# The order of value products and scores on TensorE in two attention layers with narrow heads

## The chip, the cores and the metric

The kernel is one program on one core of a Trainium2 chip. The metric is the device time in microseconds of one execution. Three runs of the kernel before took 1552.82, 1553.26 and 1553.35 us; the median is 1553.26.

## The reference

The input x is 32 sequences of 64 tokens of 256 values, and a context of the same shape. Four layers follow one another:

- L0: two cross-attentions with 16 heads of 128 values, with layer norms and residuals, then a feed-forward stage of 1024 (gelu).
- L1: cross-attention in which the keys and values come from the context and x together (128 per sequence), 16 heads of 16 values, with a mask; then an RMS norm and a feed-forward stage.
- L2: layer norm, cross-attention to the context (64 keys), 16 heads of 16 values, with a mask; then layer norm and feed-forward.
- L3: a non-local block over all tokens with a norm over the whole batch.

The two layers with narrow heads are L1 and L2. For each of them, cut to what matters:

```
q, k, v = x @ wq + bq, h @ wk + bk, h @ wv          # 16 heads of 16
scores  = where(mask, q k^T, -big) * scale
w       = softmax(scores)
x       = (w v) @ wo + bo (+ residual)
```

Most products are computed in three passes: each float32 operand is split into a high and a low part of a faster format, and the products high-high, high-low and low-high are added (`split3`).

## The kernel before, in words

Each engine runs its own program, written out in order; semaphores join them. The function `narrow(layer, ...)` writes the part of all engines for L1 and L2. Its work is cut into units. In layer 1 a unit is one sequence (NU = 32 units, 128 keys), in layer 2 it is two sequences (NU = 16, 64 keys each). A half is 256 tokens: four units in layer 1, two in layer 2 (UH). The counter r is the place of a unit in its half.

What happens to unit u, in order of its data:

1. `pe_scores(e, u)` on TensorE: four small matmuls write the mask into the four score banks (L1609), then the products of queries and keys are added (L1616). It waits for the subtraction of unit u-1 (`sub_done`), since the banks are the same.
2. VectorE takes the maximum (L1869) and subtracts it (L1873).
3. ScalarE takes the exponential (L1760).
4. VectorE sums (L1843) and takes the reciprocal (L1846), one unit later in its program.
5. POOL multiplies (L1986).
6. `pe_transpose(e, u)` on TensorE turns the probabilities into banks 4 and 5 (L1631), in the loop two units later. It waits for POOL, for the copy of the unit before out of these banks, and for each bank until its last other user is evicted.
7. ScalarE copies them out (`act_probs`, L1782); its semaphore is `p_copied`.
8. `pe_values(e, u)` on TensorE multiplies them with the values (L1648), three units later. It waits for `p_copied` of its unit and for `lo_done` of the unit before.
9. ScalarE and VectorE split the result into a high part (`act_hi`, L1796) and a low part (`dve_lo`, L1838).
10. The output product of two such units (layer 1) or of one (layer 2), and its eviction into x_sb on VectorE (L1832).

Between these, TensorE computes the projections of the halves ahead (queries q, keys kc or k0 and k1, values v), the output products ("out") and transposes of the next norm ("norm"). These are the uses of a table that `Slots` keeps: `uses_of[u]` lists those of unit u in order, and `pe_use` issues one. Each has a bank; it waits until the use before in that bank is evicted, and a use in one of the banks of the transposes (4, 5) waits also for `p_copied` of unit u-3 (`turned`). In layer 1 the banks of the uses are 7 and 5 in turn, so k0, a norm and mostly "out" come to bank 5; in layer 2 "out" takes bank 4 (in units 9, 14 and 15 bank 7). The three-pass products of all uses have the line L175. `n_ahead` is the number of uses that the loop issues in the first group: 3 in layer 1, which is all of them, and 1 in layer 2. In layer 1 the uses are q, k0 at r=0; k1, out at r=1; v, and in some units norm, at r=2; v, out at r=3. In layer 2 they are mostly kc, out, q at r=0 and v, out, sometimes norm, at r=1.

ScalarE's order in unit u: evictions of the first group of uses, `act_hi(u-3)`, the other early evictions, the exponential of u, late evictions (q of layer 2 among them, L1713), `act_probs(u-2)`, parts of the norm. VectorE's order in unit u: maximum and subtraction of u, in layer 2 `dve_lo(u-3)`, the eviction of "out", sum and reciprocal of u-1, in layer 1 `dve_lo(u-3)`, parts of the norm.

Behind the loop come the last units, mixed with the feed-forward stage's first products.

Of the kernel before, what the change touches and what calls it, by code (L numbers as in the profile page):

```python
# [86 lines left out]
def build(nc, wpack, ctxT, ctx_tok, x_in, mask1, mask2, cols_in, rows_in, vb_in, out, spill):  # L87
    ctx = ExitStack()
    with ctx:
# [70 lines left out]
        def wait(e, sem, n):  # L160

            if n > 0:
                e.wait_ge(sem, n)
# [1230 lines left out]
        def narrow(layer, norm, nxt, qb, kb, vb, out_row, mask, before, behind, then):  # L1394
# [118 lines left out]
            def out_of(use):  # L1513

                if use[0] == "norm":
                    return use[1].s["ev"].sem, use[1].s["ev"].at(use[2] * KT + use[3])
                return (A_out if use[0] in slots.ON_ACT else V_out), slots.emptied[use]
# [7 lines left out]
            def values_banks(w):  # L1525

                return BP if own or w < NU - 3 else (6, 7)
# [67 lines left out]
            def pe_scores(e, u):  # L1595
                h, r = u // UH, u % UH
                if r == 0:
                    e.wait_ge(*out_of(("q", h)))
                    e.wait_ge(*out_of(("k1" if own else "kc", h)))
                if u == 0:  # L1600
                    e.wait_ge(mask_ready, layer)
                    e.wait_ge(before.sem, before.at(NCH - 1))
                else:
                    e.wait_ge(sub_done, u)
                for j in range(G // KT):
                    cells = ps[:, j, 0:KT * P].rearrange("p (k n) -> p k n", k=KT)
                    i, at = u // (NU // 4), u % (NU // 4) * UB * SEQ
                    keys = maskb[PW * j:PW * j + 4, at:at + UB * SEQ]
                    e.matmul(cells[:, :, 0:UB * SEQ], sel[PW * j:PW * j + 4, i:i + 1].to_broadcast([4, P]),  # L1609
                             keys.rearrange("p (a n) -> p a n", a=1).to_broadcast([4, KT, UB * SEQ]),  # L1610
                             start=True, stop=False, skip_group_check=True)
                for k in range(KT):
                    for b in range(UB):
                        for j in range(G // KT):
                            at, rows_j = k * P + b * nk, slice(PW * j, PW * (j + 1))
                            ins = e.matmul(ps[:, j, at:at + nk],  # L1616
                                           qz[h % 2][rows_j, k, r * UB + b, :, :].rearrange("p h n -> p (h n)"),
                                           kT[h % 2][rows_j, k, r * UB + b, :], start=False, stop=True, skip_group_check=True)
                ins.then_inc(S_done, 1)

            def pe_transpose(e, u):
                e.wait_ge(nrm_done, u + 1)
                wait(e, p_copied, u)
                for half in range(2):
                    use = slots.last_in(BT[half], min(u + 2, NU))
                    if use is not None:
                        e.wait_ge(*out_of(use))
                    if BT[half] in BP:
                        wait(e, lo_done, min(u, NU - 3))
                    for n in range(4):  # L1630
                        ins = e.transpose(ps[:, BT[half], n * P:(n + 1) * P], t[u % 3][:, 4 * half + n, :], ident)  # L1631
                ins.then_inc(T_done, 1)

            def pe_values(e, u):
                h, r = u // UH, u % UH
                e.wait_ge(p_copied, u + 1)
                wait(e, lo_done, u)
                if u == 0:
                    e.wait_ge(*out_of(("row",)))
                e.wait_ge(*out_of(("v", h, r // 2 if own else 0)))  # L1640
                if not own and u == NU - 3:
                    e.wait_ge(*out_of(("out", last_outs[NU])))
                for k in range(KT):
                    for half in range(2):
                        for b in range(UB):
                            for j in range(G // KT):
                                rows_b = slice(b * nk, (b + 1) * nk)
                                ins = e.matmul(ps[j * PW:(j + 1) * PW, values_banks(u)[b], k * SEQ:(k + 1) * SEQ],  # L1648
                                               v[h % 2][half][rows_b, r, k * P + j * PW:k * P + (j + 1) * PW],
                                               pt[rows_b, j * KT + k, half * SEQ:(half + 1) * SEQ],  # L1650
                                               start=half == 0, stop=half == 1, skip_group_check=True)
                ins.then_inc(P_done, 1)
# [7 lines left out]
            def pe(e):  # L1660
                for use in uses_of[-1][1:]:
                    pe_use(e, -1, use)
                for u in range(NU):
                    pe_scores(e, u)
                    for use in uses_of[u][:n_ahead]:
                        pe_use(e, u, use)
                    if u >= 3:
                        pe_values(e, u - 3)
                    for use in uses_of[u][n_ahead:]:
                        pe_use(e, u, use)  # L1670
                    if u >= 2:
                        pe_transpose(e, u - 2)
                e.wait_ge(sub_done, NU)
                for use in uses_of[NU]:
                    pe_use(e, NU, use)
                then.lead(e)
                pe_transpose(e, NU - 2)
                pe_values(e, NU - 3)
# [304 lines left out]
            def pool_normalise(e, w):  # L1983
# [7 lines left out]
                          for f in range(7)}  # L1991
            behind[FT - 2] = Parts(pe_first, nothing, nothing if own else dve_columns, None)
            return load_mask, Parts(pe, act, dve, pool)

        next0, next1, next2, tail0, tail1, tail2 = Next(), Next(), Next(), {}, {}, {}
# [467 lines left out]
```

## Time and profile before

| what | value |
|---|---|
| median of three runs | 1553.26 us |
| span of the profiled execution | 1550.8 us |
| TensorE matmul (PE) busy | 1517.9 us |
| TensorE weight load (PEld) busy | 1304.4 us |
| VectorE (DVE) busy | 974.2 us |
| ScalarE (ACT) busy | 855.8 us |
| POOL busy | 402.3 us |

The profiled execution has no other time than its span of 1550.8 us, which is 2.5 us below the median of the runs. The trace puts the narrow layers at 1019.75 to 1167.21 us (the units of layer 1) and 1274.55 to 1367.46 us (those of layer 2). A row of a timeline gives start and length in us, the engine and line, how many instructions were merged, and in brackets how long the engine was idle before and which instruction ended that. The length of a matmul row has the drain of its last product in it, so that the next row can start before it ends.

### The profile page before, as it was taken

The page shows a single profiled execution, that of the slowest core. Times are in us where ns is not written, and L with a number is a line of the kernel's source. Part 1 is how long each engine was busy: PE and PEld are TensorE (multiplying, and loading weights), DVE is VectorE, ACT ScalarE, POOL GpSimd, SP SyncE. Part 2 cuts the span into 40 slices and gives each one's busy share as a digit, 9 for nine tenths or more (in the row PEclk, how much of TensorE's full clock was granted, in tenths as well). Part 3 has the DMA queues.
Part 4 walks back from the last instruction along what each step waited for, and adds up shares of the span by engine and source line. Part 5 has one row for each costly group of instructions (what it writes and reads, how often), then busy time and mean ns, then how long its engine had stood idle before and what let it go on. Part 6 is the DMA issues. An engine that isn't in the chain of part 4 may idle for free. (4 is left out here: it accounts for less than half of the span.)

```text
span 1550.8 us, 41283 instructions
## 1 busy us (share of the span) xinstructions
PE 1517.9 (98%) x17264; PEld 1304.4 (84%) x17264; DVE 974.2 (63%) x2115; ACT 855.8 (55%) x1610; POOL 402.3 (26%) x422
## 2 busy tenths in 40 slices
PE   8999999999999999999999999999999999999996
PEld 7888888888888888888888888978878988888864
DVE  7755555555577555555555576479996558865366
ACT  5553453453455453443443566576777567765476
POOL 1231011011033011101201123036764206542052
PEclk9999999999999999999999999999999999999998
DMA  6010010010010010010100000020002000000001
GB/s 229 2 70 2 29 43 1 29 42 1 29 42 2 29 42 1 29 43 1 31 27 29 28 2 28 1 84 2 3 29 83 1 28 3 31 2 28 8 22 55
DMA packets 17688, 46.20 MB, mean 30 GB/s; under 512 B 1344, under 2 KB 11600, under 8 KB 14560
## 3 DMA queue, kind: packets, MB, share of 16 engines
q1 hardware_dynamic: 13312, 39.33, 7.4%
q10 hardware_dynamic: 4192, 4.24, 0.8%
q8 instruction: 137, 2.24, 0.6%
q14 instruction: 47, 0.39, 0.1%
HBM read 39.37 MB, written 4.19 MB: 28 GB/s over the span
## 5 line engine op out<-in xcount | busy, mean ns | idle before, releaser
L175 PE MATMUL ps<-ch,W 128*128 128x512 f32 (+1 forms) x2484 | 596.5, 386 | 1.4 <-ACT arena L1725 0.6
L175 PEld LDWEIGHTS ps<-ch,W 128*128 128x128 f32 x2484 | 432.6, 188 | 87.5 <-issue 2.2
L175 PEld LDWEIGHTS ps<-W,split_arena 128*128 128x128 f32 x3084 | 392.6, 188 | 25.7 <-issue 4.2
L175 PE MATMUL ps<-W,split_arena 128*128 128x256 f32 x3084 | 406.5, 283 | 3.5 <-DVE split_arena L1226 2.4
L175 PE MATMUL ps<-W,ch 128*128 128x512 f32 (+1 forms) x864 | 203.5, 384 | 0.3
L892 ACT ACTIVATE arena<-ps 64x256 f32<-64x256 f32 x256 | 97.0, 379 | 187.8 <-PE ps L791 184.8
L991 DVE TENSOR_REDUCE small<-ps 128x4 f32<-128x260 f32 x128 | 54.1, 422 | 221.1 <-PE ps L720 221.0
L175 PEld LDWEIGHTS ps<-W,ch 128*128 128x128 f32 x864 | 151.6, 188 | 28.4 <-ACT arena L1713 0.9
L952 ACT ACTIVATE arena<-ps,hbias 128x512 f32<-128x512 f32 x128 | 87.8, 688 | 119.2 <-PE ps L175 118.3
L1226 DVE TENSOR_TENSOR split_arena<-arena,split_arena 128x512 fp32r<-128x512 f32 x96 | 71.9, 749 | 125.4 <-ACT split_arena L1258 113.8
L930 ACT ACTIVATE arena<-arena 128x260 f32<-128x260 f32 x128 | 54.3, 425 | 142.0 <-DVE arena L994 142.0
L1986 POOL TENSOR_TENSOR arena<-arena,small 128x1024 f32<-128x1024 f32 x48 | 94.9, 1979 | 126.9 <-DVE small L1846 126.9
L1255 ACT ACTIVATE arena<-ps,cols 128x512 f32<-128x512 f32 x96 | 65.9, 687 | 92.7 <-PE ps L175 92.7
L984 DVE SCALAR_TENSOR_TENSOR split_arena<-ps,hbias,split_arena 128x256 fp32r<-128x256 f32 x256 | 105.6, 474 | 0.5 <-ACT split_arena L899 0.2
L1022 DVE TENSOR_TENSOR arena<-ps,arena 128x256 f32<-128x256 f32 x128 | 54.1, 423 | 78.3 <-PE ps L175 78.0
L222 POOL COPY hbias<-raw 128x8 f32<-128x8 f32 x15 | 3.3, 221 | 379.0 <-PE ps L175 379.0
L1014 DVE TENSOR_TENSOR x_sb<-ps,x_sb 128x512 f32<-128x512 f32 x128 | 87.2, 686 | 16.4 <-PE ps L175 16.2
L899 ACT ACTIVATE split_arena<-ps,hbias 128x512 fp32r<-128x512 f32 x128 | 80.9, 683 | 26.6 <-PE ps L805 26.4
L805 PEld LDWEIGHTS ps<-arena 64*64 64x64 f32 x4096 | 65.6, 135 | 22.3 <-issue 21.8
L907 ACT ACTIVATE arena<-ps,hbias 128x512 f32<-128x512 f32 x128 | 80.0, 676 | 2.5 <-PE ps L175 2.0
L720 PE MATMUL ps<-arena 128*64 128x65 f32 x2048 | 73.8, 225 | 1.5 <-ACT arena L952 0.8
L805 PE MATMUL ps<-arena 64*64 64x64 f32 x4096 | 74.3, 221 | 0.0
(168 smaller groups left out, 1967.7 us busy)
## 6 DMA issues: line engine op xcount, KB each, us to landing
raw<-wpack SPq DMA_DIRECT2D x23, 1028.0 KB, 4.9
arena<-vb_in SPq DMA_DIRECT2D x8, 512.0 KB, 5.8
x_sb<-x_in SPq DMA_DIRECT2D x4, 512.0 KB, 9.6
arena<-ctxT SPq DMA_DIRECT2D x4, 512.0 KB, 9.9
spill<-x_sb ACTq DMA_DIRECT2D x1, 2048.0 KB, 11.4
arena<-spill ACTq DMA_DIRECT2D x1, 2048.0 KB, 8.3
arena<-ctx_tok SPq DMA_DIRECT2D x16, 128.0 KB, 2.1
out<-x_sb SPq DMA_DIRECT2D x7, 256.0 KB, 2.5
```

What stands on the lines that cost most here:

```text
L175: last = e.matmul(dst, lhs[a], rhs[b], start=start and n == 0, stop=stop and n == 2, skip_group_check=True)
L720: ins = e.matmul(ps[r:r + SEQ, BS[h], n // 2 * KEYS0:(n // 2 + 1) * KEYS0], qs[h][:, n * SEQ:(n + 1) * SEQ], ks[h][:, n, :], start=True, s ...
L805: ins = e.matmul(ps[dims, BO + b, at:at + SEQ], values[keys, h * DH0 + d * SEQ:h * DH0 + (d + 1) * SEQ], pts[h][keys, n, :], start=True, s ...
L892: ins = e.activation(pts[h][b * SEQ:(b + 1) * SEQ], own[:, :, b * SEQ:(b + 1) * SEQ], ACT.Copy)
L899: e.activation(head_split(h, 0), head_cells(h), ACT.Identity, bias=head_col(t, 3, h)).then_inc(a_oh, 1)
L907: e.activation(ks[h][:, :, key_slots(h)], cut(ps[:, h, :], BPC), ACT.Identity, bias=head_col(u, 1, h)).then_inc(a_ke, 1)
L952: e.activation(qs[h], ps[:, 2 + h, :], ACT.Identity, bias=head_col(u, 0, h)).then_inc(a_qe, 1)
L984: ins = e.scalar_tensor_tensor(head_split(h, 1)[:, :, b, :], head_cells(h)[:, :, b, :], head_col(t, 3, h), head_split(h, 0)[:, :, b, :].bi ...
L1014: e.tensor_tensor(xs, cut(ps[:, banks[j], :], 2), xs, ALU.add).then_inc(a_acc, 1)
L1226: e.tensor_tensor(gsp[f % 2][1], gelu[:, f % 2, :], gsp[f % 2][0].bitcast(F32), ALU.subtract).then_inc(s["gl"].sem, 1)
L1255: e.activation(gelu[:, f % 2, :], ps[:, f % 2, :], func, bias=col(f"fb{which}", f)).then_inc(s["gel"].sem, 1)
L1986: e.tensor_tensor(cells, cells, many(inv[w % 2], nk), ALU.mult).then_inc(nrm_done, 1)
```

## The change

In the loop of `narrow`'s TensorE program, `pe_scores(e, u)` moves from ahead of the first group of uses to behind `pe_values(e, u - 3)`. The programs of the other engines, the semaphores and the table of uses are the same.

```diff
                 for u in range(NU):
-                    pe_scores(e, u)
                     for use in uses_of[u][:n_ahead]:
                         pe_use(e, u, use)
                     if u >= 3:
                         pe_values(e, u - 3)
+                    pe_scores(e, u)
                     for use in uses_of[u][n_ahead:]:
                         pe_use(e, u, use)
                     if u >= 2:
                         pe_transpose(e, u - 2)
```

## Rows read from the trace of the kernel before

**Rows 1.** The page, engine totals: busy us (share of the span) xinstructions.
```profile
PE 1517.9 (98%) x17264; PEld 1304.4 (84%) x17264; DVE 974.2 (63%) x2115; ACT 855.8 (55%) x1610; POOL 402.3 (26%) x422
```
**Rows 2.** Windows, both stretches: length, busy us, granted clock, DMA share, GB/s.
```profile
1019.75:1167.21 147.46, 142.59 (x2276) 119.27 (x2277) 135.15 (x197) 111.30 (x191) 98.94 (x99) 1.00 0.09 30
1274.55:1367.46 92.91, 89.76 (x1880) 80.96 (x1879) 76.60 (x115) 69.80 (x122) 56.12 (x63) 1.00 0.08 26
```
**Rows 3.** Timeline of layer 1: start, length, engine, line, instruction, [idle before <-releaser].
```profile
1097.51 0.67 PE L1616 MATMUL ps<-arena 32*128 32x128 f32 x16
...
1098.26 1.22 DVE L1869 TENSOR_REDUCE small<-ps 128x8 f32<-128x1024 f32 x1 [0.97 <-PE ps L1616]
...
1099.52 1.22 DVE L1873 TENSOR_TENSOR arena<-ps,small 128x1024 f32<-128x1024 f32 x1
...
1100.41 0.65 PE L1648 MATMUL ps<-arena 128*32 128x64 f32 x32
1100.66 0.41 DVE L1832 TENSOR_TENSOR x_sb<-ps,x_sb 128x256 f32<-128x256 f32 x1
...
1101.00 1.09 PE L1631 MATMUL ps<-cols,arena 128*128 128x128 f32 x8
...
1101.31 1.05 ACT L1760 ACTIVATE arena<-arena 128x1024 f32<-128x1024 f32 x1
...
1102.03 0.23 PE L1609 MATMUL ps<-rows,small 4*128 4x128 bf16 x4
...
1102.26 1.02 ACT L1782 ACTIVATE arena<-ps 128x1024 f32<-128x1024 f32 x1
1102.35 0.24 DVE L1838 TENSOR_TENSOR split_arena<-ps,split_arena 128x128 fp32r<-128x128 f32 x1
...
1104.75 0.65 PE L1648 MATMUL ps<-arena 128*32 128x64 f32 x32
```
**Rows 4.** Timeline of layer 1, unit 28, which has no uses.
```profile
1150.57 0.65 PE L1648 MATMUL ps<-arena 128*32 128x64 f32 x32 [0.56 <-ACT arena L1782]
```
**Rows 5.** Timeline of TensorE, value products of layer 1: units 0 and 28.
```profile
1033.45 0.66 PE L1648 MATMUL ps<-arena 128*32 128x64 f32 x32
...
1165.31 0.66 PE L1648 MATMUL ps<-arena 128*32 128x64 f32 x32
```
**Rows 6.** Timeline, layer 1: v; transposes' second half; q and k0; out.
```profile
1083.82 1.70 PE L175 MATMUL ps<-W,split_arena 128*128 128x256 f32 x12
...
1091.31 0.42 PEld L1631 LDWEIGHTS ps<-cols,arena 128*128 128x128 f32 x4 [0.24 <-DVE x_sb L1832]
...
1092.57 3.07 PE L175 MATMUL ps<-ch,W 128*128 128x256 f32 x18
...
1099.61 0.88 PE L175 MATMUL ps<-W,split_arena 128*128 128x256 f32 x6
```
**Rows 7.** Timeline of layer 2, units 8 to 10.
```profile
1322.66 0.42 DVE L1832 TENSOR_TENSOR x_sb<-ps,x_sb 128x256 f32<-128x256 f32 x1
...
1324.10 1.93 ACT L1713 ACTIVATE arena<-ps,small,cols 128x256 f32<-128x256 f32 x4 [1.01 <-PE ps L175]
...
1325.90 1.04 ACT L1782 ACTIVATE arena<-ps 128x1024 f32<-128x1024 f32 x1
...
1327.70 0.86 PE L1648 MATMUL ps<-arena 64*32 64x64 f32 x64
...
1330.30 0.29 PE L1609 MATMUL ps<-rows,small 4*128 4x256 bf16 x4
...
1330.42 1.01 PE L1616 MATMUL ps<-arena 32*128 32x64 f32 x32
```
**Rows 8.** Timeline of TensorE, value products of layer 2: units 0 and 12.
```profile
1289.51 0.86 PE L1648 MATMUL ps<-arena 64*32 64x64 f32 x64
...
1364.01 0.86 PE L1648 MATMUL ps<-arena 64*32 64x64 f32 x64
```
**Rows 9.** Windows, behind the last matmul.
```profile
1540.00:1545.00 5.00, 0.00 (x0) 0.00 (x0) 4.38 (x11) 2.99 (x6) 0.39 (x1) 0.50 0.24 81
```

## The prediction

> **What bounds the kernel now.** I read first the page's engine totals: TensorE is busy 98% of the span [rows 1]. Then the two stretches that the change touches, by windows: the 32 units of the first narrow layer take 147.46 us with TensorE busy 142.59 and VectorE 135.15; the 16 units of the second take 92.91, with 89.76 and 76.60 [rows 2]. TensorE sets the pace, and at most 147.46 - 142.59 + 92.91 - 89.76 = 8.0 us of waiting can be had there. Then the timeline of single units: what each engine does behind a unit's scores, and how long TensorE leaves it for that.
>
> **Names.** S is mask and scores of unit u, A its first uses (three in layer 1, one in layer 2), B the rest, V the value products of unit u-3, T the transposes of unit u-2. Before: S A V B T. After: A V S B T. The counts and bytes are the same; no DMA, no instruction of SP, POOL, VectorE or ScalarE moves. The only gain or loss is in waits.
>
> **Why a wait is added.** V(u-3) waits for the copied probabilities of u-3. ScalarE issues that copy behind the exponential of u-1, which waits for the subtraction on VectorE and so for S(u-1). Before, TensorE had A(u-1), V, B, T, S(u) and A(u) between the end of S(u-1) and V(u-3): from 1098.18 (1097.51 + 0.67) to V at 1104.75, 6.6 us, and the copy was never late but where A is empty: there V waited 0.56 [rows 3, 4]. After, only B(u-1), T(u-3) and A(u) lie between, and S(u) stands behind V. That closes a ring: S(u-1), maximum, subtraction, exponential, copy, V, S(u).
>
> **Chain to the copy, from e, the end of S(u-1)** [rows 3]. Maximum at e+0.08 (1098.26 against 1098.18); subtraction 1.26 later, at e+1.34, done e+2.56; exponential e+2.60; copy 0.95 behind its start (1102.26 against 1101.31), e+3.54, done e+4.56 (1.02 long); TensorE goes on 0.05 to 0.15 later: e+4.64. V to the next block 0.59 (1100.41 to 1101.00), with 0.07 for a handover 0.66; mask to end of S 0.73. So V to the new e is 1.39, and the bare ring is 4.64 + 1.39 = 6.03 us per unit, against (1165.31 - 1033.45)/28 = 4.71 now [rows 5].
>
> **Layer 1, further waits in the new place.**
> - Odd units have an output product in A. Its bank belongs to the transposed probabilities, so it too waits for the copy: starts e+4.64, 0.83 long (0.88 less the drain of its last product [rows 6]), V at e+5.47, period 6.86. That lo(u-4), which it also needs, ends earlier: eviction starts e+2.48, lo is done 1.93 behind that (1102.59 against 1100.66), at e+4.41 [rows 3].
> - T in an odd unit needs that bank emptied by VectorE, behind the subtraction: e+2.48 + 0.41, its second half goes at e+2.95. Today this costs 0.24 [rows 6]; now T stands next to S. TensorE reaches A(u) at e+3.5. Where A is q and k0 (3.0 us [rows 6]), V is at e+6.5: period 7.89. Where it is v (1.62), e+5.12: 6.51; with the norm's transposes 0.44 more: 6.95.
>
> Sum of the 28 intervals V(0) to V(28): 13 odd x 6.86 = 89.2; one odd unit without the bank (u=29) 6.46; u=8 to 24 by fours 5 x 7.89 = 39.5; u=28, empty A [rows 4], 6.03; v with norm 4 x 6.95 = 27.8, without 2 x 6.51 = 13.0; u=30 6.56; u=4, whose k0 waits for the copy, 7.43. Together 196.0 against 131.86 [rows 5]: +64.1. Start: A(0) stands ahead of S(0) for 3.0 us, of which waits of units 0 to 2 give back 0.9: V(0) 2.1 later. End: behind S(31) the transposes of the last units wait for VectorE and POOL (V(28) to T(30) 7.9 against 5.96 now): +1.9. Layer 1: +68.
>
> **Layer 2.** V is 0.80 to the next block (0.86 less the drain), S 1.13 with its mask (1330.30 to 1331.43): V to e is 2.0 with the handover [rows 7].
> - Behind an even unit ScalarE evicts q between exponential and copy, 1.80 more (1324.10 to 1325.90 [rows 7]): copy done e+6.36, V e+6.46. Four such (u=7, 9, 11, 13).
> - T waits for the output's eviction: subtraction done e+2.56, lo and eviction 0.42 each (the eviction's row; lo writes as many elements), T at e+3.40, 1.03 to the next block [rows 3]; then A, 1.62: V at e+6.04. Four such (u=5, 6, 8, 12).
> - The others: u=4 6.25 (eviction of keys ahead of the copy, then the output product), u=10 5.15, u=15 5.17 (the output in another bank, T waits only for lo), u=14 5.65 (T, then the copy).
>
> 4 x 6.46 + 4 x 6.04 + 6.25 + 5.15 + 5.17 + 5.65 = 72.2, and 12 x 2.0: 96.2, against 1364.01 - 1289.51 = 74.50 [rows 8]: +21.7. Start +1.5, end +3.2 (the output of unit 12 now waits for lo behind the last subtraction). Layer 2: +26.4.
>
> The feed-forward stages behind both layers are TensorE's own work, so nothing gives this back. Sum +94.6: span 1550.8 + 94.6 = 1645.4. The median of the runs, 1553.26, lies 2.5 above the span of the profiled execution: 1648.
>
> **Bounds.** Below: only the bare ring and the output's wait bind, and T is never in the way (its transposes start early, or the eviction is hidden): layer 1 loses 5 x 1.86 + 6 x 0.8 = 14, layer 2 some 8, start and ends 7: about +65, 1618. Above: each of five handovers in a ring takes the 0.17 us of the row of the mask's load [rows 3] instead of 0.05 to 0.08, 5 x 0.1 x 40 units = 20: 1668. I take 1648, since both T waits have a row today with the same releaser. For the handover before S the row of T to mask (1.03, 0.17 of it issue) is the nearest; I used 0.07.
>
> **The clock.** It is 1.00 in both stretches [rows 2] and falls to 0.50, the 1.2 GHz level, only behind the last matmul [rows 9]. After the change TensorE is idle for about a third of the first stretch (142.6 of 216 busy) and a quarter of the second, the longest gap 2.4 us (end of S to the held T). The Trainium skill, "TensorE: Matmul & The Clock Gate", section "Why this matters for your kernels", says that idle gaps between bursts of matmuls can send the clock back to its lower level; that gives the second rival. No row of this trace shows such a gap with work behind it.
>
> **Rivals.**
> 1. The chain isn't late: TensorE stays the bound and only the order of busy work changes. For: V waits for the copy only where A is empty [rows 4]. Against: the time left to the copy falls by one S, one V and one A, to T and A, 2.7 to 4.1 us of work, where it needs 4.64. Time 1553. Chance 4%.
> 2. The clock falls in the gaps. A ring has 2.2 to 5 us of TensorE work on its path; doubled on some 44 rings, +2.5 x 44 = 110 more: about 1758. For: a third of the time idle. Against: no gap is longer than a unit's softmax. If it falls only at times, 1670 to 1700. Chance 9% for both.
> 3. Faster, by one mechanism: V earlier brings ScalarE's and VectorE's split of the heads (hi, lo) ahead of the exponential. Today the exponential starts 0.57 behind the end of the subtraction (1101.31 against 1100.74), held by the hi copy of V's result, which stands ahead of it in ScalarE's queue [rows 3]. Were this what delays the POOL's product and T, the waits of TensorE in both stretches, at most 8.0 us, would go: 1545 at best. It decides only where A alone covers 4.64 us, and the longest A is 3.0. Chance 2%.
> 4. Slower, but only by the bare ring (the lower bound): 1618. Chance 13%, against 72% for the forecast.
>
> **Range and chances.** 1648, with 1618 to 1672 for 8 in 10; it takes in the lower bound and the start of rival 2. About 0.2% (3 us) is what a measurement can tell from no change. Faster 0.03, same 0.04, slower 0.93.
>
> **What would show it.** Right: layer 1's V rows 6 to 8 us apart, 7.9 in each fourth; 216 us for its stretch and about 119 for the second's; V or the output product waiting for the ScalarE copy in nearly every unit, T half waiting for VectorE's x_sb eviction in odd units; VectorE's maximum waiting for nothing but S, 0.08 behind it; all other stages to 0.1% as now. Wrong: TensorE still above 95% busy there (rival 1), a clock below 1.00 (rival 2), or q and k0 units no longer than the others (rival 4).

## The result

| kernel | median us | runs | ratio to before, 95% |
|---|---|---|---|
| before | 1553.13 | 1552.82 to 1553.35 (4) | 1 |
| after | 1682.61 | 1676.55 to 1687.93 (4) | 1.0832 [1.0807, 1.0857] |

The change costs 129.5 us; 94.6 were forecast, and the time lies 10.6 us above the upper end of the range. The profiled execution has a span of 1679.8 us, 129.0 more than before's, and a mean granted clock of 0.965. The page of the kernel after, span, engine totals and the clock in 40 slices:

```profile
span 1679.8 us, 41283 instructions
...
PE 1558.2 (93%) x17264; PEld 1338.7 (80%) x17264; DVE 973.7 (58%) x2115; ACT 859.0 (51%) x1610; POOL 402.7 (24%) x422
...
PEclk9999999999999999999999998888879998999998
```

Against [rows 1] the counts are the same, and VectorE, ScalarE and POOL are busy nearly as long as before (at most 3.2 us off). TensorE is not: the same 17264 matmuls take 40.3 us more, since part of them runs at a lower clock, and that in the slices of the two narrow layers. The other 88.7 of the 129.0 us are idle time of TensorE (121.6 where it was 32.9), in which the forecast put its whole loss. What TensorE waited for in the kernel after (releaser, us in total, times, longest):

```profile
PE ps L1631 <- DVE x_sb L1832: 41.0, 22, 2.4
PE ps L175 <- ACT arena L1782: 28.9, 13, 2.3
PE ps L1631 <- DVE split_arena L1838: 7.0, 4, 2.4
PE ps L175 <- ACT arena L1713: 4.4, 4, 1.1
```

The first two are the forecast's two waits: transposes held by the eviction of "out" behind the subtraction, and "out" held by the copy. The timeline of the kernel after, units 11 to 15 of layer 1, cut (start, length, engine, line, instruction, idle before):

```profile
1099.11 1.00 ACT L1782 ACTIVATE arena<-ps 128x1024 f32<-128x1024 f32 x1
...
1100.21 0.95 PE L175 MATMUL ps<-W,split_arena 128*128 128x256 f32 x6 [2.21 <-ACT arena L1782]
...
1101.09 0.65 PE L1648 MATMUL ps<-arena 128*32 128x64 f32 x32
...
1101.75 0.67 PE L1616 MATMUL ps<-arena 32*128 32x128 f32 x16
...
1102.49 1.23 DVE L1869 TENSOR_REDUCE small<-ps 128x8 f32<-128x1024 f32 x1 [2.86 <-PE ps L1616]
1103.75 1.23 DVE L1873 TENSOR_TENSOR arena<-ps,small 128x1024 f32<-128x1024 f32 x1
1104.89 0.41 DVE L1832 TENSOR_TENSOR x_sb<-ps,x_sb 128x256 f32<-128x256 f32 x1
1105.01 1.06 ACT L1760 ACTIVATE arena<-arena 128x1024 f32<-128x1024 f32 x1 [2.92 <-DVE arena L1873]
...
1105.36 0.91 PE L1631 MATMUL ps<-cols,arena 128*128 128x128 f32 x4 [2.35 <-DVE x_sb L1832]
...
1105.92 4.45 PE L175 MATMUL ps<-ch,W 128*128 128x256 f32 x18
1106.31 1.02 ACT L1782 ACTIVATE arena<-ps 128x1024 f32<-128x1024 f32 x1 [0.24 <-PE ps L1631]
...
1110.30 0.65 PE L1648 MATMUL ps<-arena 128*32 128x64 f32 x32
...
1116.29 0.94 PE L175 MATMUL ps<-W,split_arena 128*128 128x256 f32 x6 [2.24 <-ACT arena L1782]
1117.16 0.65 PE L1648 MATMUL ps<-arena 128*32 128x64 f32 x32
...
1124.01 1.08 PE L1648 MATMUL ps<-arena 128*32 128x64 f32 x32
...
1131.81 0.65 PE L1648 MATMUL ps<-arena 128*32 128x64 f32 x32
```

Read it as a ring. The scores end at e = 1102.42. VectorE's maximum starts 0.07 later, the held half of the transposes goes at e+2.94 (forecast e+2.95). The odd unit behind it goes from V at 1110.30 to V at 1117.16: 6.86 us, as computed. But the 18 products of q and k0 last 4.45 us where they took 3.07 in [rows 6], so the unit of q and k0 takes 9.21 and not 7.89. The 32 value products at 1124.01 take 1.08 in place of 0.65: the same work, at a lower clock. The granted clock stands behind the counts in the windows of the kernel after (length, busy us of PE, PEld, DVE, ACT, POOL, granted clock, DMA share, GB/s):

```profile
1100.00:1105.00 5.00, 2.80 (x62) 2.24 (x62) 2.47 (x3) 0.94 (x4) 2.82 (x3) 1.00 0.00 0
1105.00:1110.00 5.00, 4.64 (x22) 4.36 (x22) 1.79 (x4) 3.21 (x5) 3.01 (x3) 0.66 0.01 3
1110.00:1115.00 5.00, 4.05 (x68) 2.92 (x66) 3.26 (x3) 2.33 (x5) 0.00 (x0) 1.00 0.00 0
...
1230.00:1235.00 5.00, 3.85 (x59) 3.06 (x60) 2.46 (x5) 2.04 (x3) 3.54 (x3) 0.50 0.01 3
...
1265.00:1365.00 100.00, 98.98 (x732) 88.92 (x733) 56.48 (x135) 61.83 (x100) 20.60 (x21) 1.00 0.09 31
```

It falls behind the gaps, for some us at a time, at 1230 down to 0.50 (1.2 GHz), and it is 1.00 throughout the feed-forward stage, where TensorE works without gaps. The block in front of layer 2's loop, first in the kernel before, then in the kernel after:

```profile
1273.66 0.96 PE L175 MATMUL ps<-W,split_arena 128*128 128x256 f32 x6
...
1368.14 0.97 PE L175 MATMUL ps<-W,split_arena 128*128 128x256 f32 x6
```

It starts 94.5 us later: layer 1 costs 94.5 of the 129.0 (68 forecast), layer 2 34.5 (26.4 forecast).

### The profile page after: what moved, and what is told of

Its sections match the earlier page's. It is cut to its first block and busy times, and to the rows that moved or that the text cites. A ratio compares the mean times of both kernels' runs of the same rounds, so it can differ in the third digit from the quotient of the medians.

```text
span 1679.8 us, 41283 instructions
## 1 busy us (share of the span) xinstructions
PE 1558.2 (93%) x17264; PEld 1338.7 (80%) x17264; DVE 973.7 (58%) x2115; ACT 859.0 (51%) x1610; POOL 402.7 (24%) x422
## 3 DMA queue, kind: packets, MB, share of 16 engines
q8 instruction: 137, 2.24, 0.5%
## 5 line engine op out<-in xcount | busy, mean ns | idle before, releaser
L175 PE MATMUL ps<-ch,W 128*128 128x512 f32 (+1 forms) x2484 | 605.4, 391 | 2.9 <-issue 2.1
L175 PEld LDWEIGHTS ps<-ch,W 128*128 128x128 f32 x2484 | 441.0, 193 | 88.6 <-issue 4.5
L175 PE MATMUL ps<-W,split_arena 128*128 128x256 f32 x3084 | 417.7, 288 | 39.8 <-ACT arena L1782 28.9
L175 PEld LDWEIGHTS ps<-W,split_arena 128*128 128x128 f32 x3084 | 400.7, 192 | 64.3 <-issue 39.1
L952 ACT ACTIVATE arena<-ps,hbias 128x512 f32<-128x512 f32 x128 | 87.8, 688 | 119.2 <-PE ps L175 118.4
L1869 DVE TENSOR_REDUCE small<-ps 128x8 f32<-128x1024 f32 (+1 forms) x48 | 58.7, 1224 | 153.2 <-PE ps L1616 153.2
L1760 ACT ACTIVATE arena<-arena 128x1024 f32<-128x1024 f32 x48 | 50.8, 1058 | 133.5 <-DVE arena L1873 133.5
L1631 PE MATMUL ps<-cols,arena 128*128 128x128 f32 x384 | 63.6, 308 | 50.4 <-DVE x_sb L1832 41.0
L1014 DVE TENSOR_TENSOR x_sb<-ps,x_sb 128x512 f32<-128x512 f32 x128 | 87.2, 687 | 16.1 <-PE ps L175 15.9
L1631 PEld LDWEIGHTS ps<-cols,arena 128*128 128x128 f32 x384 | 46.7, 155 | 62.4 <-DVE x_sb L1832 32.2
```

The lines of the kernel that those rows point to most:

```text
L175: last = e.matmul(dst, lhs[a], rhs[b], start=start and n == 0, stop=stop and n == 2, skip_group_check=True)
L952: e.activation(qs[h], ps[:, 2 + h, :], ACT.Identity, bias=head_col(u, 0, h)).then_inc(a_qe, 1)
L1014: e.tensor_tensor(xs, cut(ps[:, banks[j], :], 2), xs, ALU.add).then_inc(a_acc, 1)
L1869: e.tensor_reduce(mx[u % 2], cells, axis=AX.X, op=ALU.max).then_inc(max_done, 1)
```

## The experiments

All differences are of medians, against the runs of the kernel before on the same chip (1552.77 to 1552.98). In the loop's TensorE program, `own` is true in layer 1.

### Where: one layer at a time

```diff
+if not own: pe_scores(e, u)       # e1_layer1: new order in layer 1 alone
 ... first uses, values
-pe_scores(e, u)
+if own: pe_scores(e, u)
```

(e2_layer2 has the two conditions exchanged.)

> The new order stands in the first narrow layer only; the second keeps the order of before. Measured for both together: 1682.6 us against 1553.1. In the trace of the changed kernel the block just ahead of the second layer's loop (1273.66 us before, 1368.14 after) lies 94.5 us later and the rest of the 129.0 us, 34.5, falls behind it. Theory (the rings are local to a layer, the clock's losses too): 1553.1 + 94.5 = 1648, within 6 us for the changing clock. Rival (what one layer leaves behind, a late engine or a low clock, costs in the other): with this run and its twin for the second layer the two losses add up to 10 us or more less or more than 129.

> The new order stands in the second narrow layer only. Theory: 1553.1 + 34.5 = 1588, within 4 us. Rival: the losses of the two layers don't add up to 129 within 10 us.

Measured: layer 1 alone 1652.22 (1.0647 [1.0628, 1.0666]), +99.3; layer 2 alone 1584.79 (1.0212 [1.0195, 1.0229]), +31.9. Together 131.2 against 129.5: the layers add, within the spread of the runs, and nothing is given back between them.

### How much of it is the clock

Matmuls whose results nobody reads fill the long gaps; they go into a bank that is overwritten next.

```diff
 # in pe_use, ahead of the use
+if own and u % 2 and 5 <= u < NU and use[0] in ("k1", "v"):
+    spin(e, slots.bank[use], 6)                  # 128x512 each
+if not own and 5 <= u < NU and (use[0] == "norm" or use[0] == "q"):
+    spin(e, slots.bank[use], 5 if use[0] == "norm" else 2)
 # in pe_transpose, ahead of the first half
+if own and half == 0 and u % 2 and 3 <= u < NU - 2:
+    spin(e, BT[0], 6)
```

> The changed kernel with matmuls added that only keep TensorE busy: six of 128x512 (0.25 us each) in the first layer ahead of k1 or v in odd units and ahead of the first half of the transposes in odd units, where the trace shows gaps of 2.2 and 2.35 us; in the second layer five ahead of the norm's transposes and two ahead of q. They write into a bank that the next products overwrite. Theory (about 32 us of the 129 are the lower clock, the other 97 the rings of waits): the granted clock rises to 0.99 or more and the time falls to 1645 to 1660, with 28 intervals between the value products of the first layer of 196 to 202 us (218.1 in the changed kernel). Rival (the clock costs next to nothing, since TensorE waits anyway, and I mis-sized the rings): time 1676 or more, though the clock rises. Second rival (the added matmuls stand in the ring): slower than 1690.

Measured: 1653.99 (1653.27 to 1655.77), ratio 1.0656 [1.0638, 1.0674]. More work, 28.6 us less than the kernel after, and the mean clock is 0.991 where it was 0.965. The timeline of e3_spin, value products (line 1658 there) of units 0, 8 to 12 and 28 in layer 1, and 0 and 12 in layer 2:

```profile
1036.62 0.65 PE L1658 MATMUL ps<-arena 128*32 128x64 f32 x32 [1.83 <-ACT arena L1792]
...
1093.82 0.65 PE L1658 MATMUL ps<-arena 128*32 128x64 f32 x32
1101.50 0.65 PE L1658 MATMUL ps<-arena 128*32 128x64 f32 x32
1108.36 0.65 PE L1658 MATMUL ps<-arena 128*32 128x64 f32 x32
1114.65 0.65 PE L1658 MATMUL ps<-arena 128*32 128x64 f32 x32
1121.52 0.65 PE L1658 MATMUL ps<-arena 128*32 128x64 f32 x32
...
1233.19 0.65 PE L1658 MATMUL ps<-arena 128*32 128x64 f32 x32
...
1361.45 0.86 PE L1658 MATMUL ps<-arena 64*32 64x64 f32 x64
...
1460.00 0.86 PE L1658 MATMUL ps<-arena 64*32 64x64 f32 x64
```

With the clock mostly back, the intervals are those of the forecast: 7.68, 6.86, 6.29 and 6.87 for four units, with 7.89, 6.86, 6.51 and 6.86 computed, and 1233.19 - 1036.62 = 196.6 for the 28 intervals, with 196.0 computed. In the kernel after the same products, units 0 and 28, stand at

```profile
1037.72 0.65 PE L1648 MATMUL ps<-arena 128*32 128x64 f32 x32 [1.73 <-ACT arena L1782]
...
1255.82 1.08 PE L1648 MATMUL ps<-arena 128*32 128x64 f32 x32
```

so its 28 intervals take 218.1. The rings are there with full clock too; the clock costs about 28.6 us on top. That is rather too low than too high, since e3_spin's clock is still below 1.00 in its first and last units. The 40.3 us by which the matmuls of the kernel after are longer are an upper figure: part of that time lies in waits that stand anyway.

### Is it the place of V, or that of S

A third order, A S V B T, in both layers: the scores behind the first uses, but ahead of the values.

```diff
 for use in uses_of[u][:n_ahead]: pe_use(e, u, use)
+pe_scores(e, u)
 if u >= 3: pe_values(e, u - 3)
-pe_scores(e, u)
```

> Half of the move, in both layers: scores go behind the first group of uses but stay ahead of the value products (A S V B T). The ring of exponential, copy and value products is open, since no scores wait behind value products. Theory (what is left are the waits of uses ahead of the scores: the output product waits for the copy, the transposes for the output's eviction, v of the second layer for the eviction of q): four units of the first layer 25.8 us at full clock against 28.2 in the changed kernel and 19.1 before, so most of the loss stays: 1620 to 1655 with what the clock takes. Rival (only value products ahead of scores cost, as the ring of my prediction says): within 10 us of before, 1553 to 1563.

Measured: 1627.73 (1624.03 to 1632.84), 1.0484 [1.0459, 1.051]; +74.8. Taking V out of the way of the scores gives back 54.9 of the 129.5. Waits for the copy and for the eviction stay, shorter. The spans say what the 54.9 is made of: TensorE is busy 1533.8 us in e4_uses_scores_values, 24.4 less than in the kernel after. So of the 53.2 us between the two spans nearly half is the clock, and 28.8 are waits. The timeline of e4_uses_scores_values, layer 1:

```profile
1100.15 0.95 PE L175 MATMUL ps<-W,split_arena 128*128 128x256 f32 x6 [1.68 <-ACT arena L1782]
...
1104.71 0.66 PE L1631 MATMUL ps<-cols,arena 128*128 128x128 f32 x4 [1.77 <-DVE x_sb L1832]
```

So the larger part of the harm, 74.8, comes with moving S behind A (that brings S next to T, and "out" ahead of S), and the rest with V in between as well. That holds in this order of the two steps; V ahead of S with A behind it was not run.

### Opening the rings, one by one

Each ring can be opened on the other engines. On e1_layer1, all in layer 1 alone: ScalarE's copy ahead of the exponential (e5), VectorE's eviction and low part ahead of the maximum (e6), both (e7).

```diff
 # ScalarE, e5 and e7, ahead of the exponential
+if own and u >= 2:
+    act_probs(e, u - 2)
 # ... and behind it
-if u >= 2:
+if u >= 2 and not own:
     act_probs(e, u - 2)
 # VectorE, e6 and e7, ahead of the maximum
+if own:
+    for use in uses_of[u]:
+        dve_use(e, use)
+    if u >= 3:
+        dve_lo(e, u - 3)
```

(In e6 and e7 the two steps are taken out of their old place in layer 1.)

> The new order in the first narrow layer only (1652.2 us), and there ScalarE copies the probabilities of unit u-2 ahead of the exponential of u instead of behind it. Theory (the ring of exponential and copy is only one of two; in even units the held transposes bind, in odd ones the output product would next wait for the low part that VectorE writes at e+4.1, so that 0.44 us of each of 14 odd units go): 6 us less and a little clock, 1638 to 1648. Rival (the ring through exponential and copy is the whole loss of this layer): with the exponential out of it, back to within 25 us of before, below 1578.

> As the run before, but ScalarE's order is left, and VectorE evicts the output product and writes the low part of u-3 ahead of the maximum of u instead of behind its subtraction. Theory (the transposes are no longer held, but k0, the norm and the output product still wait for the copy at e+4.64): four units 27.4 us against 28.2 at full clock, 6 us less over the layer and the clock's share of the vanished 2.35 us gaps: 1625 to 1646. Rival (the held transposes are the main loss): below 1600.

> Both edits at once, first layer only. Theory (either ring alone keeps the loss, both open it; what is late next is POOL's product: subtraction, sum, reciprocal and product end 6.0 us behind the scores of the unit before, then transposes, copy, value products and scores 3.5: 9.5 us in two units, and with TensorE's own 4.7 us of work a period near 5.3): the layer loses 20 to 30 us instead of 99: 1573 to 1585. Rival (the gains of the two edits add up): about 1625 to 1640.

| kernel | median us | ratio to before, 95% | against e1 |
|---|---|---|---|
| e1_layer1 | 1652.22 | 1.0647 [1.0628, 1.0666] | |
| e5_copy_first | 1636.37 | 1.0537 [1.0521, 1.0553] | -15.9 |
| e6_evict_first | 1629.96 | 1.0494 [1.0478, 1.051] | -22.3 |
| e7_both_first | 1590.25 | 1.0238 [1.0222, 1.0254] | -62.0 |

Two parts give 38.2 singly and 62.0 together: they are two rings over the same units, and the one left closed keeps most of the loss. By waits alone this is plainer still. TensorE is busy 1556.2 us in e1, 1545.3 in e5, 1539.6 in e6 and 1528.3 in e7; taken off their spans (1650.0, 1632.6, 1629.0, 1590.2), its idle time falls by 6.5, 4.4 and 31.9 us, and the rest of each gain is the clock that came back. Run e5 came out 1.6 us below its expected range, e6 inside it. The waits name what kept the rings closed. TensorE's waits in e5_copy_first:

```profile
PE ps L1631 <- DVE x_sb L1837: 28.9, 17, 2.4
PE ps L175 <- DVE split_arena L1843: 18.3, 10, 2.3
```

Without the copy, "out" waits for the low part, which stands behind the same subtraction. In e6_evict_first it is the copy again: the timeline shows it done just as "out" goes, though the wait is named "issue" there. The sum of these waits, then one of them:

```profile
PE ps L175 <- issue: 35.2, 16, 2.9
...
1107.13 1.00 ACT L1785 ACTIVATE arena<-ps 128x1024 f32<-128x1024 f32 x1
...
1108.23 0.95 PE L175 MATMUL ps<-W,split_arena 128*128 128x256 f32 x6 [2.26 <-issue]
```

And in e7_both_first, TensorE's waits in the units of layer 1:

```profile
PE ps L1631 <- POOL arena L1994: 28.8, 21, 2.2
```

Both rings are open, and a third releaser holds the transposes: POOL's product, behind the sum and reciprocal. Of the 39.4 us that its span is longer than before's, 29.0 are idle time of TensorE, most of it this wait, and 10.4 are longer matmuls (the granted clock is 0.90 from 1024 to 1190). The expectation had POOL's ring in it, so it is not news that explains the 5.3 us by which e7 lies above its range; whether that ring was sized too small or the clock did it was not taken apart.

### The third ring, and its price

On e7, VectorE's sum of unit u-1 goes between maximum and subtraction of u, so that POOL starts earlier.

```diff
     # between maximum and subtraction
+    if own and u:
+        dve_sum(e, u - 1)
```

> The kernel with both edits in the first layer (1590.3 us), and in that layer VectorE sums unit u-1 between the maximum and the subtraction of u instead of behind the subtraction. In the run before this one TensorE waits 28.8 us, 21 times, for POOL's product ahead of the transposes. Theory (that is the next ring, as forecast): POOL's product comes 1.2 us earlier, the subtraction 1.2 us later, which nobody waits for any more; the waits for POOL nearly vanish and the time falls by 20 to 30 us to 1560 to 1570. Rival (the later subtraction holds the next scores, or VectorE itself is full): 1580 or more.

Measured: 1610.87 (1.0375 [1.0358, 1.0392]), 20.6 slower than e7. The POOL waits are gone, and dearer ones stand in their place. TensorE's waits in e8_sum_between:

```profile
PE ps L1609 <- DVE arena L1885: 18.2, 22, 2.4
PE ps L1631 <- ACT arena L1734: 13.3, 6, 2.9
```

The mask of the next unit waits for the subtraction, now 1.2 us later. The exponential waits for it too, and ScalarE's eviction of k0 stands behind that exponential: it is what the transposes wait for in the second row. The rival was right. The expected gain was turned into new waits.

### Layer 2

On e2_layer2: VectorE writes the low part ahead of the maximum and evicts "out" between maximum and subtraction, and ScalarE evicts q and copies ahead of the exponential.

```diff
 # VectorE
+if u >= 3 and not own: dve_lo(e, u - 3)      # ahead of the maximum
+for use in uses_of[u] if not own else (): dve_use(e, use)   # ahead of the subtraction
 # ScalarE, ahead of the exponential
+for use in uses_of[u][n_ahead:]: act_use(e, use)            # q with them, not own
+if not own and u >= 2: act_probs(e, u - 2)
```

> The new order in the second layer only (1584.8 us), and there VectorE writes the low part of u-3 ahead of the maximum and evicts the output product between maximum and subtraction, and ScalarE evicts q and copies the probabilities of u-2 ahead of the exponential of u. Theory (in this layer the held transposes and the copy behind the eviction of q are the loss): gap from scores to value products 6.3 us with q (7.15 now), 4.5 without (6.0 to 6.2 now), so some 10 us less and 3 of clock: 1568 to 1577. Rival (the exponential, now last, holds the sum, POOL's product and the transposes): no gain or slower than 1584.

Measured: 1565.43 (1.008 [1.0063, 1.0096]), 19.4 us less than e2 and 2.6 below the expected range; +12.7 is left of +31.9. Here the eviction, 0.4 us, stands ahead of the subtraction, and the three edits together still gain. TensorE's waits in e9_layer2_early:

```profile
PE ps L1631 <- POOL arena L1994: 5.9, 8, 1.9
PE ps L175 <- ACT arena L1716: 4.9, 5, 1.1
PE ps L1631 <- DVE x_sb L1838: 3.2, 5, 1.6
```

### Does any of it help the kernel before

```diff
 # c1_evict_before_lo: layer 2, VectorE: eviction of "out" ahead of dve_lo(u - 3)
 # c2_sum_between: layer 1, VectorE, as in e8
+if own and u: dve_sum(e, u - 1)
```

> The kernel before, with its order on TensorE, and one edit from the findings: in the second layer VectorE evicts the output product ahead of writing the low part. There the transposes wait for that eviction 0.17 to 0.50 us in four units. Theory: 0.5 to 1.5 us less, 1552. Rival: the low part, 0.4 us later, holds the next output product or the value products instead, no change or slower.

> The kernel before with its order on TensorE, and in the first narrow layer VectorE's sum of u-1 between maximum and subtraction of u. Before, TensorE waits about 3 us in this layer for POOL's product. Theory (that product 1.2 us earlier): 1 to 3 us less, 1550 to 1552. Rival (the subtraction 1.2 us later holds the next scores, which follow it by 0.07 to 1 us today): 5 to 20 us slower.

Measured: c1 1553.75 (11 runs), 1.0004 [0.9994, 1.0013], no change that can be told, where 0.5 to 1.5 us less was expected. In layer 2 the transposes' waits for that eviction fall from 1.0 to 0.5 us and those for the low part rise from 0.7 to 1.8, as its rival said. Run c2 gives 1569.58, 1.0107 [1.009, 1.0123], +16.8. TensorE's waits in c2_sum_between:

```profile
PE ps L1631 <- DVE x_sb L1832: 9.7, 17, 1.0
PE ps L1609 <- DVE arena L1875: 6.5, 7, 2.5
```

Putting 1.2 us of VectorE ahead of the subtraction costs even where S stands first. No version that was run beats the kernel before.

## Why the prediction was wrong

The side and the waits were right, the size was not. The failed step is the section on the clock: its term was put at nothing, and it measured 28.6 us.

- **The rings.** Right. T goes at e+2.94 (2.95 forecast), the odd unit takes 6.86 (6.86), both in the rows above. The 6.86 is exact in part by luck: of the two steps in it, e to V is 5.53 for 5.47 (1111.63 to 1117.16), and V to the new e is 1.33 for 1.39. With the clock mostly given back, the 28 intervals of layer 1 are 196.6 for a forecast 196.0. Singly, the units with q and k0 and those with v were computed 0.2 too long (7.68 and 6.29); slow first and last units make up for it in e3_spin.
- **The clock.** Wrong. The sum was made with 1.00 throughout. It was 0.965 over the span, and e3_spin puts its cost at 28.6 us of the 34.9 that are missing. The argument against rival 2 was that no gap is longer than a unit's softmax; that was true (no wait of TensorE in the kernel after is longer than 2.4 us) and did not protect. What came is the milder form of rival 2, "it falls only at times, 1670 to 1700". Its dear form, the clock down on some 44 rings, would have been +110, four times what was measured. The Trainium skill, "TensorE: Matmul & The Clock Gate", section "Why this matters for your kernels", says that idle gaps between bursts of matmuls can send the clock to its lower level; the trace agrees, with 0.66 in the window behind the wait of 2.35 us that ended at 1105.36, and 0.50 at 1230. That section names longer gaps than any of these; here the measured ones, 2.4 us at most, were enough.
- **Layer 2's v.** Missed, +0.6 in four units. The forecast had V wait for the copy behind q's eviction, at e+6.46. In fact v itself waits for q's eviction, and V stands behind v, at e+7.15. The timeline of the kernel after:

```profile
1418.89 1.07 PE L1631 MATMUL ps<-cols,arena 128*128 128x128 f32 x8 [1.02 <-DVE x_sb L1832]
1421.05 1.70 PE L175 MATMUL ps<-W,ch 128*128 128x256 f32 x12 [1.09 <-ACT arena L1713]
1422.67 0.86 PE L1648 MATMUL ps<-arena 64*32 64x64 f32 x64
```

  The row of that eviction stood in [rows 7]; that v's bank waits for it did not enter the sum. In e3_spin these four intervals are 9.07 or 9.08 for a forecast 8.46, 2.4 us in all. The 12 intervals, 1460.00 - 1361.45 = 98.6 against 96.2, differ by the same 2.4, but that is luck: the last one is 1.1 longer than computed (its matmuls ran at a lower clock; in the kernel after it is 6.88 for 7.17), and the other seven are 1.2 shorter together. T, at e+3.37, was where the forecast had it (3.40).
- **Start and ends.** Forecast 2.1 for V(0) of layer 1. It came 4.3 later (1037.72 against 1033.45), and 3.2 later in e3_spin. Part of that is the clock again. With layer 2's v and these, e3_spin's +101.1 stands against 94.6; of the difference of 6.5, 3.0 lie in the intervals and 1.1 in V(0); the other 2.4, at the ends, were not taken apart. So the 94.6 was 6.5 too low even with the clock mostly back.
- **The rivals.** Rival 1 (hidden), 3 (faster) and 4 (the bare ring alone, 1618): none. In rival 4 T would not be in the way; it is the largest wait of all, 41.0 us. The upper bound of the range held five slower handovers, which did not come (0.07 measured from S to the maximum), and not the clock, which did. Its 0.17 us is the idle time before the mask's weight load at 1102.02 in the trace before, a row that [rows 3] do not show.

## What to carry to other kernels

In a pipeline written out in order, follow one unit's chain until it comes back to the same engine, and look for every instruction that stands behind its releaser in another engine's queue and in its bank: the rings found that way gave the intervals of the two layers to 0.3% and 2.4%. Opening one of several gives little while another over the same units is closed (15.9 and 22.3 us singly, 62.0 together). Where a wait is added to the engine that was the bound, price its clock as well, also when each gap is short: one way to size it is to fill the gaps with matmuls that nobody reads. An instruction put ahead of the subtraction can hold the next unit's scores: VectorE's sum, 1.2 us, cost 20.6 and 16.8 us there, whatever it was meant to help.

## What the hardware showed unexpectedly

The granted clock went down with gaps of at most 2.4 us, about one in each unit (2.21, 2.35 and 2.24 us in the rows of units 11 to 14), and came back some 5 to 15 us later: 1.00, 0.66, 1.00 in three windows of 5 us at 1100 to 1115, and about 15 us near 0.50 from 1225 on. The 18 products behind the wait that ended at 1105.36 took 4.45 us for 3.07. It cost 28.6 us as measured with e3_spin, a fifth of the whole loss. The time follows the clock within one kernel too: the four runs of e2_layer2 are 1581.8 and 1582.4 us at a mean clock of 0.994, 1587.2 and 1587.5 at 0.989. And the spread of the runs widens with it: 11.4 us among four runs of the kernel after, 2.5 among four of e3_spin, 0.5 among four of before.
